# First x tile loaded in two halves, A loaded and transposed earlier, statistics of tile 3 moved back in a fused cross-attention and mixture-of-experts block

## The reference

```python
def fake_quant(x, scale, zp):
    q = jnp.clip(jnp.round(x / s + z), 0, 255)
    return (q - z) * s

x = x + jnp.tanh(g_xattn[0]) * jnp.matmul(fake_quant(_layernorm(x)), fake_quant(ctx_4096))
# second step, with x = _layernorm(x), xf = x as (tokens, D)
base = jnp.einsum('bsd,od->bso', x, W_base) + b_base
gate = jax.nn.softmax(xf @ W_gate.T, axis=-1)
thr = jax.nn.sigmoid(xf @ W_thr + b_thr[0]) * 0.125
w = where(gate - thr >= 0, gate - thr, 0), divided by its sum over the experts
h = jnp.einsum('nd,erd->ner', xf, A_w)
moe = jnp.einsum('ner,ne,eor->no', h, w, B_w) * 2.0
x = x + jnp.tanh(g_ffn[0]) * (base + moe)
```

## Time and profile before

| | us |
|---|---|
| runs of the kernel before, median (lowest to highest) | 189.72 (188.46 to 190.1) |
| the profiled execution | 189.72 |
| its span, first to last instruction | 187.7 |
| TensorE matmul busy | 176.3 (94%) |
| VectorE busy | 115.4 (61%) |
| ScalarE busy | 77.8 (41%) |
| GpSimd busy | 73.0 (39%) |
| TensorE's share of the chain that ended last | 68% |

### The profile page before, as it was taken

One profiled execution on the slowest core, in us unless ns is written; L12 is line 12 of the kernel. 1 busy time (PEld: TensorE's weight loads), 2 busy tenths in 40 slices (PEclk: granted clock), 3 DMA queues, 4 the chain that ended last, 5 costly groups with the idle time before them and its releaser, 6 DMA issues.

```text
span 187.7 us, 2996 instructions
## 1 busy us (share of the span) xinstructions
PE 176.3 (94%) x1108; PEld 154.3 (82%) x1114; DVE 115.4 (61%) x280; ACT 77.8 (41%) x120; POOL 73.0 (39%) x89
## 2 busy tenths in 40 slices
PE   4859999989999998999999999999999999999993
PEld 4755446668899998998954489999999999999992
DVE  1897985989588988978984465555431521521321
ACT  2399733574977937377510025023501410500300
POOL 3560023931001495499886985053500500500310
PEclk9997999999999999999999999999999999999999
DMA  6999999999040422074140000001102002002003
GB/s 222 328 391 388 383 409 410 308 387 351 17 113 0 148 75 115 16 133 134 23 143 5 0 0 3 0 0 75 40 0 112 0 0 115 2 0 112 3 0 112
DMA packets 13694, 23.82 MB, mean 127 GB/s; under 512 B 4967, under 2 KB 6375, under 8 KB 13680
## 3 DMA queue, kind: packets, MB, share of 16 engines
q1 hardware_dynamic: 13666, 23.63, 35.6%
q10 hardware_dynamic: 14, 0.00, 0.0%
HBM read 18.39 MB, written 4.19 MB: 120 GB/s over the span
## 4 chain that ended last, share of the span: by engine, by line
PE 68%; DVE 16%; ACT 5%; DMA 4%; issue 3%; POOL 2%; ACTq 1%; DVEq 0%; POOLq 0%
PE bank L843 14%; PE bank L965 13%; PE bank L967 13%; PE bank L966 13%; DVE st L600 4%; PE bank L953 3%; DVE q L630 2%; DMA rt<-in_L_xattn_x_zp_dram 2%; PE bank L925 2%; PE bank L901 2%; DMA q1T<-q 2%; PE bank L990 2%; PE bank L991 2%; PE bank L989 2%; DVE WTl L658 1%
## 5 line engine op out<-in xcount | busy, mean ns | idle before, releaser
L965 PE MATMUL bank<-WTh,lnTh 128*128 128x388 f32 (+1 forms) x192 | 67.5, 351 | 0.0
L967 PE MATMUL bank<-WTh,lnTl 128*128 128x388 f32 (+1 forms) x192 | 65.1, 339 | 0.0
L966 PE MATMUL bank<-WTl,lnTh 128*128 128x388 f32 (+1 forms) x192 | 65.0, 339 | 0.0
L965 PEld LDWEIGHTS bank<-WTh,lnTh 128*128 128x128 f32 x192 | 36.2, 189 | 0.3
L966 PEld LDWEIGHTS bank<-WTl,lnTh 128*128 128x128 f32 x192 | 36.2, 189 | 0.0
L967 PEld LDWEIGHTS bank<-WTh,lnTl 128*128 128x128 f32 x192 | 36.2, 188 | 0.0
L407 POOL TENSOR_TENSOR xs<-xs,tb 128x1024 f32<-128x1024 f32 x8 | 19.2, 2403 | 42.5 <-ACT xs L461 42.5
L843 PE MATMUL bank<-q,q1T 128*128 128x512 bf16 x122 | 29.7, 386 | 0.6 <-issue 0.3
L694 DVE SCALAR_TENSOR_TENSOR xs<-bank,con,xs 128x250 f32<-128x250 f32 (+2 forms) x24 | 13.0, 570 | 19.7 <-PE bank L991 16.0
L401 POOL TENSOR_TENSOR xs<-xs,colbc 128x512 f32<-128x512 f32 x14 | 18.0, 1312 | 17.1 <-DVE xs L644 12.0
L843 PEld LDWEIGHTS bank<-q,q1T 128*128 128x128 bf16 x128 | 12.4, 99 | 14.0 <-DVE q1T L588 0.5
(11 more groups left out here) (95 smaller groups left out, 218.5 us busy)
## 6 DMA issues: line engine op xcount, KB each, us to landing
xs<-in_x_dram SPq DMA_DIRECT2D x8, 512.0 KB, 6.8
landing<-in_ctx_dram SPq DMA_DIRECT2D x8, 512.0 KB, 10.8
ring<-in_ctx_dram SPq DMA_DIRECT2D x8, 512.0 KB, 5.8
out_dram<-xs SPq DMA_DIRECT2D x7, 512.0 KB, 2.6
ring<-in_L_ffn_W_base_dram SPq DMA_DIRECT2D x4, 512.0 KB, 13.1
landing<-in_L_ffn_W_base_dram SPq DMA_DIRECT2D x4, 512.0 KB, 15.6
ring<-in_L_ffn_A_w_dram SPq DMA_DIRECT2D x1, 512.0 KB, 12.7
ring<-in_L_ffn_B_w_dram SPq DMA_DIRECT2D x1, 512.0 KB, 4.7
```

The costliest lines, as they stand in the source:

```text
L965: mm(o, hi, WTh[:, k, a:b], start=(k == 0), stop=False, skip_group_check=True)
L966: mm(o, hi, WTl[:, k, a:b], start=False, stop=False, skip_group_check=True)
L967: ins = mm(o, lo, WTh[:, k, a:b], start=False, stop=(k == KT - 1), skip_group_check=True)
```

## The change

x tile 0 is loaded as two halves of 512 columns, each with a semaphore of its own, and the statistics of each half wait for theirs. A (`load(0)`) is issued behind context chunk 1 in place of behind chunk 7. The two halves of A, now the list `front`, are transposed by TensorE between the turning of q1 tiles 0 and 1 and behind the first product steps, in banks 1 and 2; ScalarE casts them between its two `scale_columns`, VectorE subtracts them ahead of its second `add_column`. On VectorE the second half of tile 3's statistics and its moments stand behind the copy of q1T tile 1; on ScalarE context chunk 2 goes ahead of q1 tile 3. The row sums of tiles 0 and 1 move to those of tile 2. The products of batch 0's right half take the banks of its left half and wait for those to be added to x; the banks of the other weight halves shift with that.

```diff
-    early = [("A", 0, 0), ("A", 0, 1), ("gates", 0, 0)] + [("W", o, i) for o in range(2) for i in range(NH)]
+    front = [("A", 0, 0), ("A", 0, 1)]
+    early = [("gates", 0, 0)] + [("W", o, i) for o in range(2) for i in range(NH)]
...
-        if key in early:
-            i = (5, 0, 7, 6, 5, 0, 6)[early.index(key)]
-        elif key == ("rows", 0):
-            i = 2
+        if key in front:
+            i = (1, 2)[front.index(key)]
+        elif key in early:
+            i = (7, 1, 2, 6, 1)[early.index(key)]
         elif key in late:
-            i = (5, 3, 7, 4, 5, 3, 4, 5, 3, 4, 5, 3, 4, 5)[late.index(key)]
+            i = (3, 4, 7, 5, 3, 4, 5, 3, 4, 5, 3, 4, 5, 3)[late.index(key)]
...
-            for t in range(MT):
+            for h in range(NH):
+                sp.dma_start(xs[:, 0, h * H:(h + 1) * H], x[0, 0:P, h * H:(h + 1) * H]).then_inc(x0_halves[h], 16)
+            for t in range(1, MT):
                 load_x(t)
-            for c in range(CPB):
+            for c in range(2):
                 load_own(("ctx", c))
-            for n in range(NS):
+            load(0)
+            for c in range(2, CPB):
+                load_own(("ctx", c))
+            for n in range(1, NS):
                 load(n)
...
-        def prod_bank(h, m):
-            return ((3, 4, 5, 0), (1, 2, 3, 4))[h][m]
+        def prod_bank(b, h, m):
+            return (1, 2, 3, 4)[m] if b and h else (3, 4, 5, 0)[m]
...
             affine_ctx(1)
+            affine_ctx(2)
             affine_q1(3)
-            affine_ctx(2)
...
             scale_columns(0, 0)
+            for key in front:
+                split_hi(key)
             scale_columns(0, 1)
...
-                if i == 0:
+                if i == 0 and t == 0:
+                    dve.wait_ge(x0_halves[h], 16)
+                elif i == 0:
                     dve.wait_ge(x_loaded[t], 16)
...
-            ln_moments(0, 3)
+            half_stats(0, 3, 0)
             round_q1(1)
             copy_q1T(0)
             round_ctx(0)
             copy_q1T(1)
+            ln_moments(0, 3, (1,))
             round_q1(2)
...
             half_stats(1, 0, 0)
+            for key in front:
+                split_lo(key)
             add_column(0, 1, 0)
             add_product(0, 1, 0)
-            split_lo(early[0])
             ln_moments(1, 0, (1,))
-            split_lo(early[1])
-            split_lo(early[2])
-            split_lo(early[3])
             add_product(0, 1, 1)
-            for key in early[4:]:
+            for key in early[:3]:
                 split_lo(key)
             add_product(0, 1, 2)
+            for key in early[3:]:
+                split_lo(key)
...
+                        if b == 0 and k2 == 0:
+                            pe.wait_ge(x1_part, m + 1)
...
-                        pe.wait_ge(x1_part, b * NH * MT + m - 1)
+                        pe.wait_ge(x1_part, b * NH * MT + m - 1 if b else m + 1)
...
             flip_q1(0)
-            keep_busy(6)
+            flip_weight(front[0])
             flip_q1(1)
             keep_busy(6)
             product_chunk(0, (0, 1))
+            pe.wait_ge(s_prm, 1)
+            flip_weight(front[1])
             flip_q1(2)
             product_chunk(1, (0, 1))
-            row_sums(0, (0, 1))
             flip_q1(3)
             product_chunk(0, (2,))
             product_chunk(1, (2,))
-            row_sums(0, (2,))
+            row_sums(0, (0, 1, 2))
...
-            second_half(0, {1: lambda: flip_early(0, 4),
-                            2: lambda: flip_early(4, 7)})
+            second_half(0, {1: lambda: flip_early(0, 3),
+                            2: lambda: flip_early(3, 5)})
             flip_ln(0)
+            pe.wait_ge(x1_part, NH * MT - 2)
             flip_weight(late[0])
-            pe.wait_ge(x1_part, NH * MT - 1)
             flip_weight(late[1])
             flip_weight(late[2])
-            pe.wait_ge(flip_read, read_no[early[5]] + 1)
+            pe.wait_ge(x1_part, NH * MT)
```

## The result

The changed kernel takes 193.94 us (median; 192.87 to 194.15, 4 runs) against 189.1 us (188.46 to 190.1, 4 runs): a ratio of 1.0226, 95% interval 1.019 to 1.0262. The ratio and the two profiled executions (194.01 and 189.72) both put the loss at 4.3 us, the medians put it at 4.8; the interval is 3.6 to 5.0. The text goes by 4.3, since the two profiles add up to it. The direction was foretold, the size was about half of what came, and 193.94 lies above the foretold range, which ended at 193.4.

What follows compares the result with a forecast made beforehand. It took a chain from the quantisation parameters through TensorE, then alternating TensorE, ScalarE and VectorE until 41 us, as the bound. Tile 3 +2.35, row sums +0.6, later stretch -0.8 made +2.15 on 189.7: 191.8 us, range 189.6 to 193.4.

Steps and rivals of the forecast that it cites:

- Part 1: x tile 0 in two loads: statistics begin some 0.6 us sooner, gain 0; one more SyncE issue of 0.4 us, cost 0.
- The rule on the parameters: Queues served in turn: small parameter loads could land sooner behind two half loads, tile 0 earlier, time still 191.8 us.
- Part 2: A's load moved forward lands at about 13.2 us; TensorE waits for it, turning q1 tile 1 at 14.85 instead of 13.6.
- Part 3: Tile 3's statistics behind the copy of q1T tile 1: TensorE turns tile 3 at 20.6 instead of 18.25, +2.35 us.
- The rule on the shared port pair: VectorE in 2-port mode blocks GpSimd fully: GpSimd's steps take 2.2 us, tile 3 turned at 21.0, end 0.4 us later.
- The row sums: 16 extra row sums behind tile 3's turning on TensorE, at 0.04 us each, add 0.6 us before the first column sum.
- Part 4: Second half's products reuse banks with margin 0.6 us, cost 0; tile 0's combined product waits at most 0.2 us, counted 0.
- Part 5: A's work leaves the stretch behind 31.36 us: normalising of tile 0 starts at 36.3 instead of 37.1, -0.8 us.
- A bound more, not less: Rival that A binds less: it lands at 12.5 us, tile 3 turned at 18.8, +0.35, 190.1 us; chance 0.3.
- The low clock did not come twice: Rival that TensorE's clock falls again behind 20.2 us, costing some 1.5 us more: 193.3 us; chance 0.15.

Runs made afterwards that it cites:

- e1: The changed kernel with x tile 0 in one load again: 192.48 us, ratio 1.0167 to the kernel before.
- e2: The kernel before with only x tile 0 loaded as two column halves: 191.96 us, ratio 1.0134.
- e3: The changed kernel with tile 3's statistics whole and ahead of the rounding of q1 tile 1 again: 192.91 us, ratio 1.0194 to the kernel before.
- e8: The kernel before with x tile 0 in two column halves and VectorE's two reciprocals ahead of tile 1's first statistics: 190.59 us, ratio 1.0065.
- f2: The kernel before with only A's load moved, to behind context chunk 1: 189.38 us, ratio 0.998.
- e5: The changed kernel with VectorE's differences of weight 1 ahead of the right half's third product: 193.29 us, ratio 1.0208 to the kernel before.
- f4: The changed kernel with x tile 0 in one load and both halves of A transposed behind the first products: 190.69 us, ratio 1.0063 to the kernel before.
- f3: The kernel before with 20 idle matmuls instead of 6 between the turning of q1 tiles 0 and 1: 188.71 us, ratio 0.9962.

## Why the prediction was right in direction and half in size

**Part 1, two loads, cost 0: this step failed, and it is the largest miss.** "It costs one more issue on SyncE's queue ... cost 0 too" took x tile 1's landing as given and counted only the issue. The landing moved from 5.3 to about 7.5 us. The gain that it allowed for came (tile 0's statistics start at 3.41, not 4.08) and was worth nothing, as it said. What it did not see is that tile 1's first half stands on VectorE ahead of the reciprocals; it named only the second half, which stands behind them. So a late x tile 1 holds up tile 0's coefficients. e1 prices the split at 1.1 to 1.5 us in this kernel, e2 at 2.5 in the kernel before.

The delay has two ways to tile 3, and both can be read by setting the changed kernel beside e1. The loads behind are late: x tile 1 by 2.2 us and each later one down to A by 0.7 to 0.8. And the clock rises later: with tile 0 quantised late, TensorE idles 1.86 us ahead of its 16 idle matmuls at 9.19, where e1 has no idle time, and the turning of tile 1 then takes 1.06 us in its timeline against 0.61. This holds for every profile: tile 1 is turned in 0.61 to 0.68 us in the six with x tile 0 in one load, and in 1.03 to 1.06 in the eight with it in two. Of the 1.6 us at tile 3 some 0.7 are A's landing, and 0.9 are A's transposes (1.12 against 0.66) and tile 1's turning at the lower clock.

**The rule on the parameters.** The Trainium skill, DMA: Bandwidth & Descriptors, section Queues, rings and completion order, has the engines serve their queues in turn. The prediction drew from it that the parameters may come sooner with two half loads. In the changed kernel they were there by 4.8 us (TensorE's spreading matmul) instead of 5.7, as the rule would have it, but not in every profile with the split: in e3 that matmul starts at 6.05. It was worth nothing, because the reciprocals waited for x tile 1. In e8, where they do not wait for it, half of the loss stayed.

**Part 2, A binds.** The mechanism was right, and without the split the sizes were too: A at 13.4 (foretold 13.2), tile 1 turned by 14.6 (14.85), tile 3 at 20.44 (20.6), all in e1. With the split A landed at 14.13. Context chunks later by a place cost nothing, as f2 shows.

**Part 3, tile 3's chain.** Right in order and size: from the copy of q1T tile 1 to GpSimd 1.87 us (foretold 1.86), GpSimd from 18.05 to 19.92, 1.87 us (1.8, between 1.26 and 2.20 of the earlier trace rows). The rule on the shared port pair, as the prediction put it (the Trainium skill, SBUF — State Buffer, section Who interferes with whom), would have had 2.2; its first step took 1.15 us beside two roundings, against 0.55 alone, and the others ran at their undisturbed 0.19 and 0.34, with no rounding beside them but the copy of q1T tile 2 (19.28 on VectorE). So the trace agrees with the rule for the step that overlaps, and the sum came nearer to the middle.

**The row sums.** Foretold 0.6, measured 0.4 in the chain. The term was half as large again as what came; the 16 extra row sums took 0.025 us each, not the 0.04 that I took from the weight loads.

**Part 4, the banks, cost 0.** Right for the second half's products: none of them waits. For the combined product of tile 0 it failed. "VectorE, not TensorE, is the later one there" was true, and just for that reason the new wait for the last product is not free: TensorE was done with its transposes at 45.20 and VectorE with the normalised tile's low part at 45.24, and TensorE idled 0.75 us until 45.95. The kernel before has no idle time right ahead of that product. In e5 0.60 us of it are left. No run gave the combined product another bank, so this price of 0.6 to 0.7 us is read from traces and not tested.

**Part 5, -0.8 us.** This step failed too. Normalising moved forward by 0.5, not 0.8, since weight 1's second half was turned 0.4 us later than I had worked out: it waited a little longer for its bank, and its four transposes took 0.66 us from start to last result, not 0.45. Then I had not looked at GpSimd: its work runs without a hole from 35.5 us, the third product needs the fifth of its six column terms (ready at 41.74), and the change put weight 1's differences behind that product. Instead of gaining 0.8 the later stretch lost 0.1 to 0.3. e5 gets 0.5 of it back.

**The sum, again.** Tile 3 +3.8 (foretold +2.35; 1.6 of it the split and its clock), row sums +0.4 (+0.6), the rest +0.1 (-0.8): +4.3 to +4.4 us. The forecast of +2.15 fell short by 1.6 for the split and 0.9 for the later stretch; two smaller misses of 0.2 each, in tile 3's chain and the row sums, went the other way.

**The rivals.** A bound more, not less, than foretold: in e1 it landed at 13.4, in the changed kernel at 14.1, in e3 at 14.4. The low clock did not come twice: it stayed low in one piece. In the changed kernel's timeline eight transposes take 1.04 us at 11.19, 1.06 at 15.08 and 0.62 at 18.62, and six idle matmuls 0.85 at 15.94 (0.50 at 10.37 in the kernel before), so the clock was at its lower level until some point between 15.9 and 18.6, where the kernel before had a stretch at full clock from 9.9 to 13.35. The windows of the changed kernel read a granted clock of 1.00 all the same there; durations are the safer witness. That this rival's 193.3 us is the nearest number of all to the measured time is luck: what brought the time there was the split and part 5.

**What stays open.** Why two loads of half a tile make the next tile late by 2 us: in all seven profiles with the columns split x tile 1 landed at 6.8 to 7.8, in the six in one load at 5.2 to 6.0, and in the one with the rows split at 6.8. That it happens is shown; by what mechanism is not. And the 0.63% that f4 leaves are not split further: tile 3's statistics, A's transposes, the row sums and the combined product's bank share them.

## What to carry to other kernels

A load that is split for an earlier start must be judged by when the loads behind it land, not by its own bytes: here the next tile came 2 us later, and it cost 1.1 to 2.5 us. Before a piece of work moves ahead of a critical one, compare its load's landing (issue plus time to landing, with its new place in the queue) with the moment at which the critical one can start; behind a wait of an in-order engine everything is late, the work of other engines too. A bank that a later step takes over brings a wait with it: price it by when the reader of its last content is done, also where another engine is the late one. And where the trace shows an idle hole ahead of a low-clock stretch, try cheap matmuls in the hole first: here they gained 0.4% (f3), and moving real work lost 2.3%.

## What the runs showed of the hardware that I had not expected

- Two column halves in place of one load: x tile 1 issued at 1.6 instead of 1.2 us, landing at 7.6 instead of 5.3 in the typical profile.
- Fourteen more idle matmuls of 128 columns, on an engine that had nothing else to do, took 0.7 us (by the ratio) to 0.8 (by the median) off the time; the runs then lay within 0.54 us (12 runs), against 1.5 in f2 (12) and 2.0 in the kernel before (23).
- Row sums with one column out each follow one another in the chain at 0.024 us (24 in 0.58).
- In the changed kernel x tile 1 landed 2.2 us later than in e1, but each load behind it, down to A, only 0.7 to 0.8 us later.
